# Two query heads projected between the first score fills of the next group, in the banks of the sums (layer 1 attention)

## The chip, the cores and the metric

The kernel runs on one core of one Trainium2 chip (trn2). The metric is the device time of one launch in microseconds (us). The kernel before has a median of 1783.52 us over 3 runs (1783.41 to 1785.67).

## What is computed

A network of two layers on 1024 tokens of 512 features. Layer 0 is an attention with 32 heads of 16 features and one shared key and value, beside a feed-forward part with weights from look-up tables. The change lies in layer 1, in its attention:

```
q = (x @ wq.T) as 32 heads of 128        # 8 key/value groups, 4 query heads to each
k = (x @ wk.T) as  8 heads of 128
v = (x @ wv.T) as  8 heads of 128
q = q * cos + rotate_half(q) * sin       # rotary positions, k likewise
scores = q k^T / sqrt(128), scaled by key in the first 128 keys, causal
attn = softmax(scores) @ v
out = attn @ wo.T                        # added to the input, with a gated feed-forward part behind it
```

All in float32. A matrix product is made of three products of a high and a low part of each operand (`products`, line 68).

## The kernel before

Layer 1's attention (`layer1`, line 1171) goes through the 8 key/value groups one after the other; queries come in 8 tiles of 128 tokens, heads in 2 pairs. A written list of steps sets the order of the work, and every engine walks the same list (`walk`, line 1250), each doing its own part of a step: `first_steps` (line 1138) once, then `group_steps(True)` (line 1105) seven times in a hardware loop, then `group_steps(False)`. Each engine works its own queue in order and waits on semaphores.

The steps that matter here are these, with the engines that carry them.

- `proj` f (line 1338): one of 12 projections of a group, 128 rows of weights by 512 tokens, 12 matmuls on TensorE (PE). f 0 and 1 are the key, 2 and 3 the value, 4 to 11 the four query heads, two halves of the tokens each. The result lies in PSUM bank f % 4. VectorE (DVE) rotates it (`rope`, lines 1519 to 1535: three operations that read the bank, then a sum in SBUF); GpSimd (POOL) splits the sum into a high and a low part (`rotated`, lines 1598 to 1621) and counts `kq_ready`. For the value, ScalarE (ACT) copies the bank instead (line 1467).
- `vturn` (line 1428): four transposes of the value on PE, split by ACT and DVE.
- `qk` n (line 1363), called `qknext` where it belongs to the next group: one fill of scores, for one tile and one head. Fill n lies in the two banks from 2 * (n % 2) on, so scores use banks 0 to 3 in turn, as the projections do. DVE takes the maximum (line 1546; for tile 0 a product and a maximum, lines 1549 and 1551), ACT the exponential (line 1503), DVE the reciprocal of the sum (line 1583), POOL the scaling (lines 1648 and 1649).
- `turn`, `av` (lines 1394 and 1406): probabilities are transposed in banks 4 and 5 and multiplied with the value; the sums lie in banks 6 and 7.
- `out` (line 1418): the output product of one tile, added to the residual by DVE (line 1576).
- `w`, `wo`: POOL splits a chunk of weights that the SyncE queue has loaded (line 1591).

ACT and DVE do what follows a score fill two steps late (`late_step`), POOL its scaling too. The first six score fills of the next group, n = 0 to 5, are tile 7 heads 0 and 1, tile 0 heads 0 and 1, tile 7 heads 2 and 3. At the end of a group the list read: projections 0 to 5 spread in the last pair of tiles but one, 6 to 11 in the last pair, then `out`, both `vturn`, six `qknext`, `out`. What a score fill waits for:

```
if n >= 2:
    pe.wait_ge(exp_ready, g * NHEADS + (n - 1))
else:
    pe.wait_ge(rope_read, g * 10 + 10)
    pe.wait_ge(vt_ready, g * 2 + 2)
pe.wait_ge(kq_ready, g * 10 + (2 * h + 4))
```

`exp_ready` says that the exponential has read the two banks, `rope_read` that rotations have read theirs, `kq_ready` that the rotated and split halves are there: fills of head h need 2 * h + 4 of the group's ten.

Of the kernel before, what the change touches and what calls it, by code (L numbers as in the profile page):

```python
# [25 lines left out]
ST, DT, BLK = S // P, D // P, 512  # L26
# [41 lines left out]
def products(pe, out, left, right, first, last):  # L68

    (lh, ll), (rh, rl) = left, right  # L70
    pe.matmul(out, lh, rh, start=first, stop=False)  # L71
    pe.matmul(out, lh, rl, start=False, stop=False)  # L72
    return pe.matmul(out, ll, rh, start=False, stop=last)  # L73
# [1024 lines left out]
AHEAD = 3  # L1098
NPAIR, NUNIT, NHEADS = len(PAIRS), len(UNITS), 2 * len(PAIRS)
NCHUNK, NFILL = 2 + G1, NB * (2 + G1)  # L1100
ROT_STEPS = 4 + 9
NTOK = len(PAIRS) // 2


def group_steps(more):

    turns = [("turn", u) for u in range(NUNIT)]
    main = [[] for _ in PAIRS]
    for u, (j, k) in enumerate(UNITS):
        main[j].append(("av", u))  # L1110
        if u + 2 < NUNIT:
            main[j].append(turns[u + 2])
    out = [("wo", i) for i in range(G1)] + turns[:2]
    for j in range(NPAIR):
        side = []
        if j + AHEAD < NPAIR:
            side += [("qk", 2 * (j + AHEAD)), ("qk", 2 * (j + AHEAD) + 1)]
        q, r = divmod(j, 4)
        if r == 0 and q:
            side.insert(0, ("out", 2 * q - 2))  # L1120
            side.insert(2, ("out", 2 * q - 1))
        if more and 4 <= j < 4 + W_RING:
            side.append(("w", j - 4))
        if more and j >= NPAIR - 2:
            half = NFILL // 2
            for f in range((j - NPAIR + 2) * half, (j - NPAIR + 3) * half):
                side.append(("proj", f))
                if f % NB == NB - 1 and f // NB + W_RING < NCHUNK:
                    side.append(("w", f // NB + W_RING))
        out += interleave(main[j], side)  # L1130
    out.append(("out", NTOK - 2))
    if more:
        out += [("vturn", 0), ("vturn", 1)] + [("qknext", n) for n in range(2 * AHEAD)]
    out.append(("out", NTOK - 1))
    return out


def first_steps():

    out = [("w", c) for c in range(W_RING)]  # L1140
    for f in range(NFILL):
        out.append(("proj", f))
        if f % NB == NB - 1 and f // NB + W_RING < NCHUNK:
            out.append(("w", f // NB + W_RING))
    return out + [("vturn", 0), ("vturn", 1)] + [("qknext", n) for n in range(2 * AHEAD)]


BANK_KINDS = ("turn", "vturn", "out")
# [22 lines left out]
def layer1(nc, a, keep):  # L1171
    ctx = ExitStack()
    with ctx:
# [3 lines left out]
        def sem(name):  # L1177
            return ctx.enter_context(nc.semaphore(name))

        resid, xth, xtl = keep["resid"], keep["xth"], keep["xtl"]  # L1180
        identf, identb, masku = keep["identf"], keep["identb"], keep["masku"]
        ps = ctx.enter_context(nc.psum_tensor("ps1", [P, 8, 512], F32))

        def bank(b):
            return ps[:, b % 8, :]
# [26 lines left out]
        proj_filled, rope_read, vt_ready = sem("proj_filled"), sem("rope_read"), sem("vt_ready")  # L1212
# [4 lines left out]
        o_high, o_low, y_added = sem("o_high"), sem("o_low"), sem("y_added")  # L1217
# [9 lines left out]

        def length(j):
            return PAIRS[j][0] + 1

        def pbuf(n):

# [39 lines left out]
        def split_count(s, g):  # L1272

            if isinstance(g, int) and g < 0:
                return place_first.split[s]
            return g * SPLIT_GROUP + (SPLIT_FIRST + place_of(g).split[s])
# [58 lines left out]
        def _(pe):  # L1335
            norm.tensor(nc, pe, range(EARLY))

            def proj(f, g):
                c, b = divmod(f, NB)
                if isinstance(g, int) and g == 0 and f == 1:  # L1340
                    norm.tensor(nc, pe, range(EARLY, ST))
                    pe.wait_ge(norm.low_ready, ST)
                if f < 4:
                    if isinstance(g, int) and g == 0:
                        if f == 0:
                            pe.wait_ge(norm.low_ready, ST // NB)
                    else:
                        pe.wait_ge(exp_ready, g * NHEADS)
                elif f < 6:
                    pe.wait_ge(rope_read, g * 10 + (f - 3))  # L1350
                elif f < 8:
                    pe.wait_ge(vt_ready, g * 2 + (f - 5))
                else:
                    pe.wait_ge(rope_read, g * 10 + (f - 5))
                if b == 0:
                    pe.wait_ge(w_split, g * CHUNKS + (c + 1))
                for d in range(DT):
                    w = (wh[:, c % W_RING, d * P:(d + 1) * P], wl[:, c % W_RING, d * P:(d + 1) * P])
                    last = products(pe, bank(f % 4), w, (xth[:, d, b * BLK:(b + 1) * BLK], xtl[:, d, b * BLK:(b + 1) * BLK]),
                                    d == 0, d == DT - 1)  # L1360
                last.then_inc(proj_filled, 1)

            def qk(n, g):
                j, i = divmod(n, 2)
                t, p = PAIRS[j]
                h = 2 * p + i
                if n >= 2:
                    pe.wait_ge(exp_ready, g * NHEADS + (n - 1))
                else:
                    pe.wait_ge(rope_read, g * 10 + 10)  # L1370
                    pe.wait_ge(vt_ready, g * 2 + 2)
                pe.wait_ge(kq_ready, g * 10 + (2 * h + 4))
                q = (qth[:, h, t * P:(t + 1) * P], qtl[:, h, t * P:(t + 1) * P])
                out = qk_banks(n)
                width = (t + 1) * P
                for c0 in range(0, width, BLK):
                    w = max(2 * P, min(BLK, width - c0))
                    k = (k0h[:, 0:w], k0l[:, 0:w]) if t == 0 else (kth[:, c0:c0 + w], ktl[:, c0:c0 + w])
                    products(pe, out[:, c0:c0 + w], q, k, True, c0 + BLK < width)
                pe.matmul(out[:, t * P:(t + 1) * P], identb[:], masku[:], start=False, stop=True).then_inc(qk_filled, 1)  # L1380

            def bank_free(s, g):
# [6 lines left out]
                if past[0] == "out":  # L1389
                    pe.wait_ge(y_added, g * NTOK + (past[1] + 2 - (0 if i >= 2 else NTOK)))  # L1390
                else:
# [14 lines left out]
            def av(u, g):  # L1406
                j, k = UNITS[u]
                t = PAIRS[j][0]
                if k == 0:
                    pe.wait_ge(o_low, g * NPAIR + max(1, j))  # L1410
                pe.wait_ge(low_ready, split_count(("turn", u), g) + 1)
                for kk in range(k, min(k + 2, t + 1)):
                    c = 2 * P * (kk - k)
                    last = products(pe, ps[:, 6 + j % 2, 0:2 * P], (vh[:, kk, :], vl[:, kk, :]),
                                    (ptnh[:, u % PT_RING, c:c + 2 * P], ptnl[:, u % PT_RING, c:c + 2 * P]), kk == 0, kk == t)
                last.then_inc(av_unit, 1)
# [92 lines left out]
        def _(dve):  # L1509
# [9 lines left out]
            def rope(f, g):  # L1519

                gg = g + 1
                r = f if f < 2 else f - 2
                c = HD1 ** -0.5 if f >= 4 else 1.0
                dve.wait_ge(proj_filled, gg * NFILL + (f + 1))
                if r >= 2 or not isinstance(gg, int):
                    dve.wait_ge(kq_ready, gg * 10 + (r - 1))
                cols = slice(f % NB * BLK, (f % NB + 1) * BLK)
                src = bank(f % 4)
                nc.vector.scalar_tensor_tensor(out=rota[:, r % 2, :], in0=src, scalar=c, in1=cos[:, cols], op0=ALU.mult, op1=ALU.mult)
                nc.vector.scalar_tensor_tensor(out=rotb[0:64, r % 2, :], in0=src[64:128, :], scalar=c, in1=sin[64:128, cols],  # L1530
                                               op0=ALU.mult, op1=ALU.mult)
                nc.vector.scalar_tensor_tensor(out=rotb[64:128, r % 2, :], in0=src[0:64, :], scalar=c, in1=sin[0:64, cols],  # L1532
                                               op0=ALU.mult, op1=ALU.mult).then_inc(rope_read, 1)
                dve.wait_ge(rope_read, gg * 10 + (r + 1))
                nc.vector.tensor_tensor(rota[:, r % 2, :], rota[:, r % 2, :], rotb[:, r % 2, :], ALU.add).then_inc(rotated_ready, 1)
# [53 lines left out]
        def _(pool):  # L1589
# [8 lines left out]
            def rotated(f, gg):  # L1598
# [9 lines left out]
                def chained(ins, n):  # L1608
                    ins.then_inc(rot_step, 1)
                    pool.wait_ge(rot_step, gg * ROT_STEPS + (base + n))  # L1610

# [521 lines left out]
```

## Time and profile before

| | |
|---|---|
| runs, median (lowest to highest) | 1783.52 us (1783.41 to 1785.67) |
| the profiled execution's own time | 1786.48 us |
| its span, first to last instruction | 1784.4 us |
| mean granted TensorE clock | 0.971 |
| PE busy | 1653.3 us (93%) |
| DVE busy | 1122.4 us (63%) |
| POOL busy | 812.6 us (46%) |
| ACT busy | 708.3 us (40%) |

The profiled execution took 2.08 us more than its span, and 2.96 us more than the median of the runs. PE's busy share counts a matmul from its start to the modelled end of its result, so successive matmuls overlap. Where an engine sat idle, a row of the trace says in square brackets for how long and whose instruction released it.

### The profile page before, as it was taken

Reading aid. Unit: us, or ns where it says so; the run is one execution under the profiler, and the core shown is the slowest. Engines: PE = TensorE matmul, PEld = TensorE weight load, DVE = VectorE, ACT = ScalarE, POOL = GpSimd, SP = SyncE. Lnnn points to the kernel's source line nnn. Section 1 sums busy time; section 2 is a strip of 40 time slices with the busy share of each in tenths; the row PEclk is TensorE's granted clock in tenths of the full one; section 3 lists DMA queues with packets and bytes.
Section 4 is the critical chain, followed back from the end, with each engine's and each line's share of the span. In section 5 each row is a group of like instructions: output and inputs, shape, how many; then the busy total and the mean of one; then the engine's idle time right before and its main releaser. Section 6 shows DMA issues by size and latency. Waiting matters only on the chain. (4 is left out here: it accounts for less than half of the span.)

```text
span 1784.4 us, 32078 instructions
## 1 busy us (share of the span) xinstructions
PE 1653.3 (93%) x10959; PEld 1276.0 (72%) x10959; DVE 1122.4 (63%) x1951; ACT 708.3 (40%) x1483; POOL 812.6 (46%) x806
## 2 busy tenths in 40 slices
PE   6767999999789999999999999999999999989999
PEld 4433444448568878878878878878878878867887
DVE  7867788604666676676576576576676676644333
ACT  4424556671135335325325325425325415432221
POOL 4089999100463363364364354355255264234331
PEclk9878999999899999999999999999999999989999
DMA  6540000000210000001001001001001002012101
GB/s 127 61 59 3 2 2 2 2 8 7 69 30 19 13 25 25 12 19 30 10 17 35 3 17 42 1 19 42 1 19 36 7 18 54 1 48 61 47 14 48
DMA packets 36417, 47.08 MB, mean 26 GB/s; under 512 B 12117, under 2 KB 18485, under 8 KB 36261
## 3 DMA queue, kind: packets, MB, share of 16 engines
q1 hardware_dynamic: 36282, 45.11, 10.6%
q8 instruction: 105, 1.72, 0.4%
q14 instruction: 30, 0.25, 0.0%
HBM read 37.56 MB, written 2.10 MB: 22 GB/s over the span
## 5 line engine op out<-in xcount | busy, mean ns | idle before, releaser
L1558 DVE TENSOR_TENSOR ptnl<-ps,ptnh 128x512 fp32r<-128x512 f32 (+1 forms) x320 | 203.8, 637 | 135.8 <-ACT ptnh L1476 130.1
L1476 ACT ACTIVATE ptnh<-ps 128x512 fp32r<-128x512 f32 (+1 forms) x320 | 177.6, 555 | 268.3 <-PE ps L1402 265.1
L71 PE MATMUL ps<-xth,wh 128*128 128x512 f32 (+1 forms) x560 | 225.5, 403 | 5.7 <-POOL wl L2019 4.1
L73 PE MATMUL ps<-xth,wl 128*128 128x512 f32 (+1 forms) x560 | 222.6, 398 | 0.0
L72 PE MATMUL ps<-xtl,wh 128*128 128x512 f32 (+1 forms) x560 | 222.4, 397 | 0.0
L904 DVE TENSOR_REDUCE negm<-ps 128x1 f32<-128x256 f32 (+12 forms) x224 | 178.2, 819 | 59.1 <-PE ps L473 51.3
L1546 DVE TENSOR_REDUCE negm<-ps 128x1 f32<-128x768 f32 (+3 forms) x224 | 183.4, 819 | 33.8 <-PE ps L1380 31.1
L71 PE MATMUL ps<-ptnh,vh 128*128 128x256 f32 x576 | 183.8, 319 | 10.3 <-DVE ptnl L1558 9.8
L715 ACT ACTIVATE pt<-ps 128x512 f32<-128x512 f32 x226 | 131.4, 597 | 91.8 <-PE ps L506 63.8
L73 PE MATMUL ps<-ptnh,vl 128*128 128x256 f32 x576 | 161.3, 280 | 0.0
L72 PE MATMUL ps<-ptnl,vh 128*128 128x256 f32 x576 | 160.7, 279 | 0.0
L1648 POOL TENSOR_SCALAR pshort<-pshort,rinv 128x128 f32<-128x128 f32 (+3 forms) x64 | 34.1, 532 | 275.2 <-DVE rinv L1583 275.2
L1075 POOL TENSOR_SCALAR onehot<-idx,lutl 128x512 f32<-128x512 bf16 x64 | 127.8, 1997 | 69.3 <-DVEq L890 62.9
L71 PE MATMUL ps<-kth,qth 128*128 128x512 f32 (+2 forms) x352 | 140.1, 398 | 5.0 <-DVE rot L1532 2.7
L1648 POOL TENSOR_SCALAR plong<-plong,rinv 128x1024 f32<-128x1024 f32 (+3 forms) x64 | 61.4, 960 | 178.1 <-DVE rinv L1583 178.1
L1503 ACT ACTIVATE plong<-ps,negm 128x1024 f32<-128x1024 f32 (+3 forms) x128 | 121.9, 952 | 43.8 <-DVE negm L1546 42.7
L1402 PE MATMUL ps<-identf,plong 128*128 128x128 f32 x832 | 128.7, 274 | 4.0 <-DVE resid L1576 2.1
L506 PE MATMUL ps<-qstack,kstack 124*128 124x512 bf16 x288 | 108.8, 397 | 24.9 <-DMA qstack<-mrows 21.9
L71 PEld LDWEIGHTS ps<-xth,wh 128*128 128x128 f32 (+1 forms) x560 | 106.4, 190 | 28.9 <-DVE hid L1974 2.4
L71 PEld LDWEIGHTS ps<-ptnh,vh 128*128 128x128 f32 x576 | 109.7, 191 | 22.5 <-DVE ptnl L1558 16.9
L73 PE MATMUL ps<-kth,qtl 128*128 128x512 f32 (+2 forms) x352 | 125.8, 357 | 0.0
L72 PE MATMUL ps<-ktl,qth 128*128 128x512 f32 (+2 forms) x352 | 125.5, 357 | 0.0
(227 smaller groups left out, 3838.8 us busy)
## 6 DMA issues: line engine op xcount, KB each, us to landing
raw<-in_w SPq DMA_DIRECT2D x48, 256.0 KB, 2.6
raw<-in_wo SPq DMA_DIRECT2D x32, 256.0 KB, 2.6
qstack<-qpart SPq DMA_DIRECT2D x40, 128.0 KB, 7.0
raw<-in_gate_main SPq DMA_DIRECT2D x10, 256.0 KB, 2.7
raw<-in_up_main SPq DMA_DIRECT2D x10, 256.0 KB, 2.8
raw<-in_down_main SPq DMA_DIRECT2D x10, 256.0 KB, 2.7
resid<-in_x SPq DMA_DIRECT2D x4, 512.0 KB, 5.4
out<-resid SPq DMA_DIRECT2D x8, 256.0 KB, 2.0
```

Of the source, the lines that this page charges most:

```text
L71: pe.matmul(out, lh, rh, start=first, stop=False)
L72: pe.matmul(out, lh, rl, start=False, stop=False)
L73: return pe.matmul(out, ll, rh, start=False, stop=last)
L506: last = pe.matmul(out, kstack[0:T_ROWS, tri(t) + kt * P:tri(t) + (kt + 1) * P], q, start=True, stop=kt != t)
L715: nc.scalar.activation(pt[:, m % PT0, :], ps[:, score_bank(m, t), :], ACT.Exp).then_inc(exp_done, 1)
L904: nc.vector.tensor_reduce(negm[:, t % 2, bass.ds(h, 1)], ps[:, m_bank(t, j):m_bank(t, j) + 4 // m_slots(t), :].rearrange("p b c -> p (b c) ...
L1075: nc.gpsimd.tensor_scalar(onehot[:], idx[:, ot * D:(ot + 1) * D], float(c), lutl[:, ot, c:c + 1], ALU.is_equal, ALU.mult).then_inc(hot_mad ...
L1402: last = nc.tensor.transpose(ps[:, b, (2 * (kk - k) + i) * P:(2 * (kk - k) + i + 1) * P], pbuf(2 * j + i)[:, kk * P:(kk + 1) * P], identf[:])
L1476: nc.scalar.activation(ptnh[:, i % PT_RING, 0:w], ps[:, b, 0:w], ACT.Copy).then_inc(high_ready, 1)
L1503: nc.scalar.activation(pbuf(n), src, ACT.Exp, bias=negm[:, n:n + 1], accum_out=rowsum[:, n:n + 1]).then_inc(exp_ready, 1)
L1546: nc.vector.tensor_reduce(negm[:, i:i + 1], qk_banks(i)[:, 0:(t + 1) * P], AX.X, ALU.max, negate=True).then_inc(max_ready, 1)
L1558: nc.vector.tensor_tensor(ptnl[:, i % PT_RING, 0:w], ps[:, b, 0:w], ptnh[:, i % PT_RING, 0:w].bitcast(F32), ALU.subtract).then_inc(low_rea ...
```

## The change

The projections of the third and fourth query head (f = 8 to 11) leave the spread in the last two pairs of tiles; the eight that stay are spread four and four. The four go between the first score fills of the next group, and their results go to banks 6 and 7, in which the sums of `av` lie, with f % 2. The score fills 0 and 1 wait only for the rotations that read their own banks, and the first two `av` of a group wait for the ten rotations. `rope` reads the new banks; the rest follows from the list.

```
+NFIRST = NFILL - 4

+def last_projections():
+    out = [("qknext", 0), ("vturn", 0), ("proj", NFIRST), ("vturn", 1)]
+    for n in range(1, 4):
+        out += [("qknext", n), ("proj", NFIRST + n)]
+    return out + [("qknext", n) for n in range(4, 2 * AHEAD)]
...
-            half = NFILL // 2
+            half = NFIRST // 2
...
-        out += [("vturn", 0), ("vturn", 1)] + [("qknext", n) for n in range(2 * AHEAD)]
+        out += last_projections()
...
+        def proj_bank(f):
+            return ps[:, f % 4 if f < NFIRST else 6 + f % 2, :]
...
                 elif f < 8:
                     pe.wait_ge(vt_ready, g * 2 + (f - 5))
+                elif f < NFIRST + 2:
+                    pe.wait_ge(o_low, g * NPAIR + 1)
                 else:
-                    pe.wait_ge(rope_read, g * 10 + (f - 5))
+                    pe.wait_ge(rope_read, g * 10 + (f - 3))
...
                 else:
-                    pe.wait_ge(rope_read, g * 10 + 10)
-                    pe.wait_ge(vt_ready, g * 2 + 2)
+                    pe.wait_ge(rope_read, g * 10 + (2 * n + 4))
...
                     pe.wait_ge(o_low, g * NPAIR + max(1, j))
+                    if j < 2:
+                        pe.wait_ge(rope_read, g * 10 + 10)
```

`first_steps` is changed alike: projections 0 to 7, then `last_projections`.

On PE, at the end of a turn of the loop, the fifth score fill (n = 4) stood behind the fourth. Before (L1380 is the mask that ends a fill, L71 to L73 the three products):

```order
L1380 MATMUL ps<-masku,identb 128x128
L1368 REGISTER_ALU
L1372 REGISTER_ALU [waits exp_ready]
L71 MATMUL ps<-kth,qth 128x512 [waits kq_ready]
L72 MATMUL ps<-ktl,qth 128x512
L73 MATMUL ps<-kth,qtl 128x512
L71 MATMUL ps<-kth,qth 128x512
L72 MATMUL ps<-ktl,qth 128x512
L73 MATMUL ps<-kth,qtl 128x512
L1380 MATMUL ps<-masku,identb 128x128
L1368 REGISTER_ALU
L71 MATMUL ps<-kth,qth 128x512 [waits kq_ready,exp_ready]
```

Of the change, the same place:

```order
L73 MATMUL ps<-xth,wl 128x512
L1383 REGISTER_ALU
L71 MATMUL ps<-kth,qth 128x512 [waits kq_ready,exp_ready]
L72 MATMUL ps<-ktl,qth 128x512
L73 MATMUL ps<-kth,qtl 128x512
L71 MATMUL ps<-kth,qth 128x512
L72 MATMUL ps<-ktl,qth 128x512
L73 MATMUL ps<-kth,qtl 128x512
L1394 MATMUL ps<-masku,identb 128x128
L1383 REGISTER_ALU
L1386 REGISTER_ALU [waits exp_ready]
L71 MATMUL ps<-kth,qth 128x512 [waits kq_ready]
```

The last matmul of projection 11 now stands directly ahead of fill 4, and fill 5, whose `kq_ready` counts all ten halves, is one fill behind it.

On DVE, the rotation of projection 11 was followed by the residual, the two halves of the value and the first maxima. Before, from the rotation's last operation on:

```order
L1535 TENSOR_TENSOR rot<-rot 128x512 [waits rope_read]
L1574 REGISTER_ALU
L1576 TENSOR_TENSOR resid<-ps,resid 128x512 [waits y_added,bank_filled]
L1553 REGISTER_ALU
L1562 TENSOR_TENSOR vl<-ps,vh 128x512 [waits bk_high]
L1553 REGISTER_ALU
L1562 TENSOR_TENSOR vl<-ps,vh 128x512 [waits bk_high]
L1544 ISA
L1546 TENSOR_REDUCE negm<-ps 128x1 [waits qk_filled]
L1544 REGISTER_ALU
L1546 TENSOR_REDUCE negm<-ps 128x1 [waits qk_filled]
```

Of the change, from the last operation of the rotation of projection 10 to that of projection 11:

```order
L1551 TENSOR_TENSOR rot<-rot 128x512 [waits rope_read]
L1560 REGISTER_ALU
L1565 TENSOR_TENSOR pshort<-ps,tscale 128x128 [waits qk_filled]
L1566 ISA
L1567 TENSOR_REDUCE negm<-pshort 128x1 [waits max_step]
L1540 REGISTER_ALU
L1545 SCALAR_TENSOR_TENSOR rot<-ps,raw 128x512 [waits kq_ready,proj_filled]
L1546 SCALAR_TENSOR_TENSOR rot<-ps,raw 64x512
L1548 SCALAR_TENSOR_TENSOR rot<-ps,raw 64x512
L1550 REGISTER_ALU
L1551 TENSOR_TENSOR rot<-rot 128x512 [waits rope_read]
```

The product and the maximum of fill 3 now stand between these two rotations, and four of the six fills' maxima ahead of the last rotation.

## Rows read from the trace of the kernel before

**Rows 1.** The page: busy time (share of the span) and instructions of each engine.
```profile
PE 1653.3 (93%) x10959; PEld 1276.0 (72%) x10959; DVE 1122.4 (63%) x1951; ACT 708.3 (40%) x1483; POOL 812.6 (46%) x806
```

**Rows 2.** Waits of PE in one turn of the loop: us in total, times, longest.
```profile
PE ps L71 <- ACT plong L1503: 1.9, 2, 1.0
PE ps L71 <- DVE ptnl L1558: 0.7, 2, 0.4
PE ps L1433 <- DVE resid L1576: 0.7, 1, 0.7
PE ps L1402 <- DVE resid L1576: 0.3, 1, 0.3
```

**Rows 3.** Timeline of PE at that turn's end: start, us, instruction [idle before <-releaser].
```profile
642.43 0.60 PE L1433 MATMUL ps<-identf,rot 128*128 128x128 f32 x4
643.68 0.66 PE L1433 MATMUL ps<-identf,rot 128*128 128x128 f32 x4 [0.65 <-DVE resid L1576]
644.09 0.48 PE L71 MATMUL ps<-kth,qth 128*128 128x512 f32 x1
...
648.35 0.39 PE L71 MATMUL ps<-k0h,qth 128*128 128x256 f32 x1 [1.04 <-ACT plong L1503]
...
649.87 0.39 PE L71 MATMUL ps<-k0h,qth 128*128 128x256 f32 x1 [0.82 <-ACT plong L1503]
...
650.37 0.47 PE L71 MATMUL ps<-kth,qth 128*128 128x512 f32 x1
...
651.88 0.48 PE L71 MATMUL ps<-kth,qth 128*128 128x512 f32 x1
...
656.29 0.60 PE L1402 MATMUL ps<-identf,plong 128*128 128x128 f32 x4
```

**Rows 4.** Timeline of DVE and POOL there: projection 11's rotation, its split, a scaling.
```profile
640.18 0.68 DVE L1529 SCALAR_TENSOR_TENSOR rot<-ps,raw 128x512 f32<-128x512 f32 x1
...
642.29 0.73 DVE L1535 TENSOR_TENSOR rot<-rot 128x512 f32<-128x512 f32 x1
...
643.25 0.62 POOL L1620 TENSOR_SCALAR qth<-rot 128x512 fp32r<-128x512 f32 x1 [0.77 <-DVE rot L1535]
...
643.95 1.30 POOL L1621 TENSOR_TENSOR qtl<-rot,qth 128x512 fp32r<-128x512 f32 x1
...
651.49 1.12 POOL L1648 TENSOR_SCALAR plong<-plong,rinv 128x1024 f32<-128x1024 f32 x1 [6.25 <-DVE rinv L1583]
```

**Rows 5.** Timeline of DVE: what follows a fill of tile 0.
```profile
649.08 0.29 DVE L1549 TENSOR_TENSOR pshort<-ps,tscale 128x128 f32<-128x128 f32 x1 [0.51 <-PE ps L1380]
...
649.40 0.29 DVE L1551 TENSOR_REDUCE negm<-pshort 128x1 f32<-128x128 f32 x1
```

**Rows 6.** Timeline of PE at another turn's end: first transposes of value and probabilities.
```profile
1186.21 0.60 PE L1433 MATMUL ps<-identf,rot 128*128 128x128 f32 x4
...
1201.58 0.60 PE L1402 MATMUL ps<-identf,plong 128*128 128x128 f32 x4
```

**Rows 7.** Stretches: us, busy time by engine, granted clock (PEclk), DMA share, GB/s.
```profile
507.70:511.50 3.80, 3.80 (x13) 2.74 (x12) 2.22 (x3) 1.20 (x2) 1.28 (x2) 0.55 0.00 0
522.40:526.00 3.60, 3.60 (x30) 3.56 (x31) 1.62 (x3) 1.20 (x2) 3.52 (x5) 1.00 0.02 5
1193.00:1197.00 4.00, 3.38 (x10) 2.44 (x10) 1.09 (x5) 1.50 (x6) 1.47 (x2) 0.60 0.00 0
```

**Rows 8.** Timeline of PE ahead of the loop: projection 8, value, first score, first sum.
```profile
491.35 0.39 PE L71 MATMUL ps<-xth,wh 128*128 128x512 f32 x1
...
502.50 1.04 PE L1433 MATMUL ps<-identf,rot 128*128 128x128 f32 x8
...
506.20 0.50 PE L71 MATMUL ps<-kth,qth 128*128 128x512 f32 x1 [2.67 <-DVE rot L1532]
...
522.39 0.39 PE L71 MATMUL ps<-ptnh,vh 128*128 128x256 f32 x1 [2.88 <-DVE ptnl L1558]
```

**Rows 9.** Timeline of DVE: one sum of a rotation that took longer than its like.
```profile
630.11 1.56 DVE L1535 TENSOR_TENSOR rot<-rot 128x512 f32<-128x512 f32 x1
```

More of the change, by code:

```diff
@@ L1140, in first_steps @@
     out = [("w", c) for c in range(W_RING)]
-    for f in range(NFILL):
+    for f in range(NFIRST):
         out.append(("proj", f))
@@ L1144, in first_steps @@
             out.append(("w", f // NB + W_RING))
-    return out + [("vturn", 0), ("vturn", 1)] + [("qknext", n) for n in range(2 * AHEAD)]
+    return out + last_projections()
 BANK_KINDS = ("turn", "vturn", "out")
@@ L1358, in proj @@
                     w = (wh[:, c % W_RING, d * P:(d + 1) * P], wl[:, c % W_RING, d * P:(d + 1) * P])
-                    last = products(pe, bank(f % 4), w, (xth[:, d, b * BLK:(b + 1) * BLK], xtl[:, d, b * BLK:(b + 1) * BLK]),
+                    last = products(pe, proj_bank(f), w, (xth[:, d, b * BLK:(b + 1) * BLK], xtl[:, d, b * BLK:(b + 1) * BLK]),
                                     d == 0, d == DT - 1)
@@ L1527, in rope @@
                 cols = slice(f % NB * BLK, (f % NB + 1) * BLK)
-                src = bank(f % 4)
+                src = proj_bank(f)
                 nc.vector.scalar_tensor_tensor(out=rota[:, r % 2, :], in0=src, scalar=c, in1=cos[:, cols], op0=ALU.mult, op1=ALU.mult)
```

## Prediction

> **What bounds the kernel now.** Read the page first: TensorE is busy for 93% of the span, no other engine for more than 63% [rows 1], and its mean granted clock is 0.971 of full. So time is gained only where PE stands still or its clock falls. Then PE's waits over one turn of the group loop: of some 136 us ((1186.21 - 642.43) / 4 [rows 3, 6]) the three largest sorts take 3.3, 1.9 for ACT's exponential and 0.7 twice for DVE [rows 2]. The timeline of the turn's end shows where they lie: the second `vturn` waits 0.65 us for the residual, score fills 2 and 3 wait 1.04 and 0.82 us for the exponentials that must read their banks [rows 3]. These are what the moved projections could fill.
>
> **What is removed, in each of seven turns.** From the first `vturn` (642.43) to fill 4 (650.37) PE spends 7.94 us [rows 3]. The work in it, by start-to-start times of the same rows: eight transposes at 0.41 a four (643.68 to 644.09), 0.82; fills 0 and 1 like fill 4, 1.51 (650.37 to 651.88), 3.02; fills 2 and 3 at 0.50 (649.87 to 650.37), 1.00. Together 4.84, so the stalls cost 3.10 us, a little over the 2.51 that the brackets show because a result's last part no longer overlaps the next matmul. With a projection of 2.79 us ((502.50 - 491.35) / 4 [rows 8]) ahead of each of fills 1 to 4 the maxima and exponentials are done in time, and the residual long before the second `vturn`. I take the whole 3.10 as gone; at least the 0.82 of the single wait on fill 3 must go, since its cover alone is 2.79.
>
> **What is added: fill 5 waits for the last projection.** Fill 5 is tile 7 of head 3 and needs all ten halves rotated and split. Projection 11 was followed on PE by an output product, two `vturn` and five fills; now only fill 4 stands between. The chain from projection 11 is in the rows: its rotation starts on DVE at 640.18, its sum ends at 643.02, POOL takes it up 0.23 later at 643.25 and ends the low half at 645.25, in all 5.07 us [rows 4]. To it come 0.16 us from PE's last issue slot to the end of its result (a matmul of 0.39 us issued 0.23 apart, 2.79 / 12), about 0.2 for the hand-offs from PE to DVE and from POOL to PE (an estimate by the 0.23 from DVE to POOL), and DVE's lateness. DVE has between the two last projections a rotation of 2.84 and the two short operations on fill 3, 0.61 [rows 5], 3.45 in all, against 0.50 + 2.79 = 3.29 on PE: late by about 0.1 to 0.2. Sum 5.07 + 0.16 + 0.2 + 0.1 = 5.5; fill 4 covers 1.51. **The new wait is 4.0 us.** At the least it is 3.7 (no lateness, hand-offs of nothing), at the most 4.8 (below, the collision). Queued behind it on PE are fill 5, the last `out` and the whole next group; nobody can pass.
>
> Waits: 4.0 - 3.10 = +0.9 us a turn, times 7 = **+6.3**, with 3.7 and 4.8 **+4.2 to +11.9**, as far as the old stalls go whole.
>
> **The clock.** In the turn at 1186 the granted clock was 0.60 over four microseconds [rows 7], part of it at the lower of the two levels, 1.2 GHz, after the same stalls of about 1 us; the stretch from the first `vturn` to the next group's first transposes took 15.37 us against 13.86 in the turn at 642 [rows 3, 6], so a fall costs 1.51. One turn in seven shows it. Ahead of the loop PE stood 2.67 us, and the clock was 0.55 right after; after another stand of 2.88 us it was 1.00 [rows 7, 8]. A single wait of 4.0 us is longer than all of these, so I take a fall in six turns of seven, five more than now: **+7.5**. Bounds: no fall at all, -1.5; in all seven, +9.1. [...]
>
> **Ahead of the loop.** From projection 8's start to the first `av` the kernel takes 31.04 us (491.35 to 522.39 [rows 8]). Its work: four projections 11.15, eight transposes 0.82, six fills 7.04, two `turn` 0.82, 19.8; the rest is waits and a clock that falls there. Afterwards the same stretch begins right behind projection 7: fill 0's halves are split while projections 6 and 7 run, so 19.8, the 4.0 for fill 5, and some 3.2 ahead of the first `av`, which hangs on fill 5's exponential in ACT's queue, as it did (2.88 and the unoverlapped part): 27.0. One or two falls of 1.51 bring 28.5 or 30.0. Against 31.04 that is -2.5 to -1.0; with two long waits there I take **-1.5**, bounds -3 and 0.
>
> **At no cost.** The `turn` and `av` of the last two pairs lose two projections each as cover; four stay in each, 11.2 us against a round trip whose stalls elsewhere are 0.4 at most [rows 2]. If it failed, 0.4 a turn. POOL's scaling of the first pair, 2 x 1.12 [rows 4], now stands between the splits of projections 9 and 10; the split of 10 ends some 0.8 late, but 11's sum arrives about 0.5 after that. Projection 8 waits for sums read before projection 6's rotation. Weight chunks, DMAs and matmuls are as many as before.
>
> **Sum.** 6.3 + 7.5 - 1.5 = +12.3 us; all low ends together give -0.3, all high ends +21.0. The profiled execution has a span of 1784.4 and 2.08 around it: 1786.48 becomes 1798.8. That execution is 2.96 above the median of the runs, so the forecast for the median is 1783.52 + 12.3 = **1795.8**. Changes below 0.2% (3.6 us) can't be told from none.
>
> **Rivals.** (1) *The clock holds.* The wait comes but the chip lets the clock stand, as after the 2.88 us [rows 8]: 6.3 - 1.5 with at most one fall as now, 1788, between no change and slower. For it speaks that one row, against it the two falls after shorter stands.
> (2) *A collision of DVE and POOL.* One sum in SBUF took 1.56 us [rows 9] instead of 0.73 [rows 4]; I take it that it met POOL's low half, which works on SBUF too. Rotation 11's sum meets the end of POOL's split of 10; if it waits out a whole such operation, each chain is 0.83 longer: +5.8, 1802. By the order above the overlap is only about 0.3.
> (3) *Faster: the wait is paid back.* While PE stands 4.0 us, ACT, DVE and POOL clear what they are behind, and the stalls early in the next group vanish. Those are 1.0 us in three waits, for `ptnl` and the residual [rows 2], with unoverlapped parts of 0.2 each (as 3.10 against 2.51 above) 1.6. It decides where more than 0.7 a turn comes back and no more turns fall (6.3 - 1.5 over seven); with all of it 1783.5 + 6.3 - 1.5 - 11.2 = 1777. Against it: those are round trips from PE over ACT and DVE back to PE [rows 2], which start after the wait and are not arrears.
>
> **Chances and range.** Forecast with most turns falling 0.68, clock holds 0.14, collision 0.10, paid back 0.08. The forecast's own span is 1790 to 1799. The range takes in half of rival 1 and the nearer part of rival 2: **1786.5 to 1801**. Faster is rival 3, 0.08; within 0.2% (up to 1787.1) is the better part of rival 1, 0.12; slower is 0.80.
>
> **What would show it.** Right: in each turn PE's L71 of a fill sits idle some 3.7 us released by POOL's low half of a query, the exponential's 1.9 and the residual's 0.65 are gone from PE's waits, and the granted clock is under 1 behind most of these waits. Wrong: a wait at fill 5 well under 3 us, or a full clock behind it.

## The result, and the profile after

| | before | after |
|---|---|---|
| runs side by side, median (lowest to highest) | 1783.95 us (1783.41 to 1785.67) | 1809.81 us (1807.22 to 1810.72) |
| ratio of the two over all runs, 95% interval | | 1.0141 (1.0123 to 1.0158) |
| the profiled execution's own time | 1786.48 us | 1809.05 us |
| its span | 1784.4 us | 1807.3 us |
| mean granted TensorE clock | 0.971 | 0.964 |

The change costs 25.9 us, where 12.3 were forecast: slower, as said, but twice as much, and 1809.81 lies above the range.

The page of the kernel after, busy time of each engine, shows no new work: the counts of instructions are the same. POOL and DVE gain 3.4 and 1.6 us, and some of their instructions do take longer where they meet (below); PE gains 6.7 us net, with matmuls that last longer at the lower clock [rows 1].

```profile
PE 1660.0 (92%) x10959; PEld 1284.2 (71%) x10959; DVE 1124.0 (62%) x1951; ACT 709.1 (39%) x1483; POOL 816.0 (45%) x806
```

PE's waits in one turn of the loop of the kernel after (us in total, times, longest) answer to rows 2. The exponential's 1.9 and the residual's 0.7 ahead of the second `vturn` are gone, as forecast. (The 0.2 for `pshort` is one in the middle of the group, which stood there before, too.) In their place stands one wait of 4.4 for POOL's low half of a query, alike in all seven turns.

```profile
PE ps L71 <- POOL qtl L1637: 4.4, 1, 4.4
PE ps L71 <- DVE ptnl L1574: 0.8, 2, 0.4
PE ps L1416 <- DVE resid L1592: 0.3, 1, 0.3
PE ps L71 <- ACT pshort L1519: 0.2, 1, 0.2
PE ps L1416 <- POOL plong L1665: 0.2, 1, 0.2
```

The timeline of PE at a turn's end of the kernel after, from fill 4 (start, us, instruction, idle before and its releaser), shows both halves of the price. Fill 5 starts 4.43 us late, and its first matmul takes 0.80 instead of the 0.48 of [rows 3]. From fill 5 to the next group's first transposes pass 6.95 us (1069.90 to 1076.85), where the kernel before needed 4.41 (651.88 to 656.29 [rows 3]) for the same fill and `out`. The wait is the same in all seven turns; that second stretch takes 5.99 us in the first turn and 6.78 to 7.01 in the others.

```profile
1063.84 0.40 PE L71 MATMUL ps<-kth,qth 128*128 128x512 f32 x1
...
1065.24 0.23 PE L1394 MATMUL ps<-masku,identb 128*128 128x128 bf16 x1
1069.90 0.80 PE L71 MATMUL ps<-kth,qth 128*128 128x512 f32 x1 [4.43 <-POOL qtl L1637]
1070.50 0.63 PE L72 MATMUL ps<-ktl,qth 128*128 128x512 f32 x1
...
1072.72 0.78 PE L71 MATMUL ps<-woh,oth 128*128 128x512 f32 x1
...
1076.85 0.60 PE L1416 MATMUL ps<-identf,plong 128*128 128x128 f32 x4
1077.80 0.66 PE L1416 MATMUL ps<-identf,plong 128*128 128x128 f32 x4 [0.35 <-DVE resid L1592]
```

Stretches of the kernel after (us, busy time by engine, granted clock, DMA share, GB/s) say why. PE is never idle from 1069.90 to 1076.90, and yet the granted clock is 0.60; over the first five microseconds it is 0.50, which is the lower of the two levels, 1.2 GHz, throughout. It was 0.50 already over the last microsecond of the wait, in which PE did nothing.

```profile
1068.80:1069.80 1.00, 0.00 (x0) 0.00 (x0) 0.07 (x1) 0.97 (x1) 1.00 (x1) 0.50 0.00 0
1069.90:1076.90 7.00, 7.00 (x20) 5.20 (x21) 1.22 (x1) 1.33 (x4) 0.65 (x2) 0.60 0.02 5
1070.00:1075.00 5.00, 5.00 (x12) 3.61 (x13) 1.22 (x1) 0.77 (x2) 0.55 (x2) 0.50 0.03 7
```

**Where the time lies.** The two traces are laid side by side by four marks: the start of Layer 1 (its second projection, the first that stands behind all the transposes of the input, 471.72 before and 470.61 after; what lies ahead of it is called Layer 0 here), the first `av` (522.39 and 520.55), the first transposes at the end of the loop's first turn (656.29 and 657.46) and of its last (1473.58 and 1496.63).

| stretch | before | after | difference |
|---|---|---|---|
| Layer 0 | 471.72 | 470.61 | -1.1 |
| Layer 1 ahead of the loop | 50.67 | 49.94 | -0.7 |
| first turn | 133.90 | 136.91 | +3.0 |
| six turns | 817.29 | 839.17 | +21.9 |
| last group and what follows | 310.82 | 310.67 | -0.1 |

Layer 1 alone is 24.0 us longer (1336.7 against 1312.7). That is the change's price in these two executions, free of what Layer 0 does, which the change doesn't touch.

### The profile page after: what moved, and what is told of

Same layout as the page of the kernel before. It is cut to its first block and busy times, and to the rows that moved or that the text cites. A ratio compares the mean times of both kernels' runs of the same rounds, so it can differ in the third digit from the quotient of the medians.

```text
span 1807.3 us, 32113 instructions
## 1 busy us (share of the span) xinstructions
PE 1660.0 (92%) x10959; PEld 1284.2 (71%) x10959; DVE 1124.0 (62%) x1951; ACT 709.1 (39%) x1483; POOL 816.0 (45%) x806
## 3 DMA queue, kind: packets, MB, share of 16 engines
q1 hardware_dynamic: 36282, 45.11, 10.3%
## 5 line engine op out<-in xcount | busy, mean ns | idle before, releaser
L71 PE MATMUL ps<-xth,wh 128*128 128x512 f32 (+1 forms) x560 | 228.3, 408 | 5.7 <-POOL wl L2035 4.1
L73 PE MATMUL ps<-xth,wl 128*128 128x512 f32 (+1 forms) x560 | 223.0, 398 | 0.0
L71 PE MATMUL ps<-ptnh,vh 128*128 128x256 f32 x576 | 184.3, 320 | 9.2 <-DVE ptnl L1574 8.7
L71 PE MATMUL ps<-kth,qth 128*128 128x512 f32 (+2 forms) x352 | 141.0, 400 | 39.1 <-POOL qtl L1637 36.7
L73 PE MATMUL ps<-ptnh,vl 128*128 128x256 f32 x576 | 161.3, 280 | 0.0
L73 PE MATMUL ps<-kth,qtl 128*128 128x512 f32 (+2 forms) x352 | 127.8, 363 | 0.0
L71 PEld LDWEIGHTS ps<-xth,wh 128*128 128x128 f32 (+1 forms) x560 | 106.8, 191 | 28.2 <-DVE hid L1990 2.4
L71 PEld LDWEIGHTS ps<-ptnh,vh 128*128 128x128 f32 x576 | 109.7, 190 | 21.3 <-DVE ptnl L1574 16.0
```

## The experiments

One theory, that the whole loss lies between fills 4 and 5 (the wait and the clock behind it), was set against three rivals: the banks and the cover that the change took from other steps; POOL's scaling in the way of the splits; and something that no row had named. Two sets of four kernels were run, each beside the kernel before (medians 1785.18 and 1785.34). Ratios are to those. Layer 0 is the same code in all of them, yet in the profiled executions it ended anywhere from 464.05 to 471.72 us. So the length of Layer 1 in each one's profiled execution, from the mark above to the end of the span, is read beside the medians. For the kernel before it is that of the one trace of it, which was not taken beside these sets:

| kernel | median, us | against before | Layer 1, us | against before |
|---|---|---|---|---|
| before | 1785.18, 1785.34 | | 1312.7 | |
| e1_filler | 1804.96 | +19.8 | 1337.7 | +25.0 |
| e2_four_ahead | 1784.71 | -0.5 | 1311.2 | -1.5 |
| e3_out_as_cover | 1778.9 | -6.3 | 1312.3 | -0.3 |
| e4_reordered | 1762.78 | -22.4 | 1296.3 | -16.4 |
| e5_filler_in_loop | 1792.57 | +7.2 | 1322.7 | +10.0 |
| e6_eight_fillers | 1798.46 | +13.1 | 1328.2 | +15.5 |
| e7_scaling_late | 1798.91 | +13.6 | 1328.9 | +16.2 |
| e8_change_again | 1808.8 | +23.5 | 1338.8 | +26.1 |

**e1_filler: keep PE at work during the wait.** Sixteen matmuls whose result is not used stand ahead of fill 5, in the loop and ahead of it; they wait until the last rotation but one has read bank 6.

```
                 elif kind == "qknext":
+                    if i == 5:
+                        pe.wait_ge(rope_read, (g + 1) * 10 + 9)
+                        for _ in range(16):
+                            pe.matmul(bank(6), qth[:, 0, 7 * P:8 * P], kth[:, 0:BLK], start=True, stop=True)
                     qk(i, g + 1)
```

> Sixteen matmuls of 512 columns, some 3.7 us, whose result nobody uses, stand between score fills 4 and 5, in bank 6 behind the rotation that reads it; nothing else differs from the changed kernel. Theory (a wait of 4.6 us at fill 5 and, behind it, a clock at the lower level that costs 2.5 us a turn): the halves are ready when they were, fill 5 starts at the same time, but PE has been busy and the clock stays up, so 7 x 2.5 and about 1 ahead of the loop come back: 1809.8 - 19 = 1791. Rival (only the wait costs, the slow stretch is hidden or comes anyway): 1810.

Measured: 1804.96 us, ratio 1.0108 (1.008 to 1.0135), far from what was expected. The timeline of PE of e1 shows that the expected part did come: fill 5 waits 0.80, and the way to the transposes is 4.42 us (645.62 to 650.04), at the full clock. But the second four transposes then stand still for 2.09 us that the profile puts down to issue, which is to say that PE waited for nothing that it shows.

```profile
645.62 0.50 PE L71 MATMUL ps<-kth,qth 128*128 128x512 f32 x1 [0.80 <-POOL qtl L1641]
...
650.04 0.60 PE L1416 MATMUL ps<-identf,plong 128*128 128x128 f32 x4
652.73 0.66 PE L1416 MATMUL ps<-identf,plong 128*128 128x128 f32 x4 [2.09 <-issue]
```

That gap, 2.09 to 2.46 us, came six times, at each start of the loop's body but the first, and slow matmuls followed it. It took back what the fillers had saved. So e1's time does not speak to the theory; e5 asks again without the code ahead of the loop.

**e2_four_ahead: the change's banks and its 4 + 4 spread, the old place.** The list at the group's end is projections 8 to 11, `out` 6, both `vturn`, fills 0 to 5, `out` 7.

> The four projections stay in banks 6 and 7 with their new waits, and the last two pairs of tiles keep four projections each, but all four stand ahead of the output product and the score fills, none between them. Theory (the loss is fill 5's wait alone): that wait goes, the old stalls of 3.1 us a turn at the second turn of the value and at fills 2 and 3 return, a clock that falls about as rarely as before: 1784 to 1787. Rival (banks 6 and 7, or the two projections that the last pairs lost as cover, cost part of the 25.9 us): 1790 or more.

Measured: 1784.71 us, ratio 0.9994 (0.9982 to 1.0007), no difference, as expected. PE's waits in one of its turns are those of the kernel before, and one new one of 0.3, of a projection for the rotation that must read its bank.

```profile
PE ps L71 <- ACT plong L1514: 1.9, 2, 1.0
PE ps L71 <- DVE ptnl L1569: 0.8, 2, 0.4
PE ps L1444 <- DVE resid L1587: 0.5, 1, 0.5
PE ps L71 <- DVE rot L1543: 0.3, 1, 0.3
```

A turn takes 136.3 to 136.4 us, some 0.4 more than the 135.97 of before's turns without a fall. That Layer 1 is 1.5 us shorter all the same lies elsewhere: no turn has a fall, and the last group and what follows take 2.5 less. So the banks 6 and 7 and the thinner spread under the last two pairs cost at most 0.4 us a turn, under 3 of the 24. The loss is the new place among the fills.

**e3_out_as_cover: something useful behind projection 11.** The list is fill 0, `vturn` 0, projection 8, fill 1, projection 9, fill 2, projection 10, fill 3, projection 11, fill 4, `out` 6, `vturn` 1, fill 5, `out` 7.

> The changed kernel with the output product and the second turn of the value moved from ahead of the fills to between fills 4 and 5. Theory (what was short is cover behind projection 11): 3.1 us more of work stand in the wait, 4.6 falls to 1.0 to 1.6, PE's other stalls at the turn's end stay gone, and so short a wait brings a fall in no more than one or two turns of seven: 1.5 to 2 us a turn under the kernel before, 1770 to 1775. Rival (projections between the fills delay maxima and exponentials on DVE whatever stands where): 1795 to 1810.

Measured: 1778.9 us, ratio 0.9969 (0.9958 to 0.998): faster than before by the medians, if by less than expected. Layer 1 does not show a gain of that size: in its one trace it is as long as in the one of before, so where the 6.3 us lie stays open. The timeline of PE of e3 shows the wait at fill 5 down to 1.17, and why the rest was missed: `out` 6 had also covered fill 0, which now waits 1.37 for its own halves.

```profile
899.72 0.47 PE L71 MATMUL ps<-kth,qth 128*128 128x512 f32 x1 [1.37 <-POOL qtl L1632]
...
916.72 0.50 PE L71 MATMUL ps<-kth,qth 128*128 128x512 f32 x1 [1.17 <-POOL qtl L1632]
```

No turn has a fall behind the 1.17. A turn takes 135.8 to 136.0 us, as before, where the change took 139.9: the old stalls are gone, and two new waits of 2.5 together stand in their place.

**e4_reordered: cover on both sides.** The list is projection 8, fill 0, projection 9, fills 1 and 2, `vturn` 0, projections 10 and 11, fill 3, `out` 6, fill 4, `vturn` 1, fill 5, `out` 7.

> The same steps in another order: projection 8, fill 0, projection 9, fills 1 and 2, first turn of the value, projections 10 and 11, fill 3, output product, fill 4, second turn of the value, fill 5, output product. Theory: behind projection 11 stand fill 3, an output product, fill 4 and four transposes, 0.5 + 2.8 + 1.5 + 0.4 = 5.2 us against a chain of 5.5 to 6.1, so the wait at fill 5 falls to 0.3 to 0.9 and the others are gone; 2.2 to 2.8 us a turn under the kernel before: 1763 to 1769. Rival (the order shifts the wait to fills 1 or 2): 1775 or more.

Measured: 1762.78 us, ratio 0.9883 (0.9855 to 0.991), as expected and ahead of both kernels. PE's waits in one of its turns list none for a projection's split (0.1 us is idle ahead of fill 5), and 0.4 of the exponential's 1.9:

```profile
PE ps L71 <- DVE ptnl L1569: 0.8, 2, 0.4
PE ps L71 <- ACT plong L1514: 0.4, 1, 0.4
PE ps L1411 <- DVE resid L1587: 0.3, 1, 0.3
```

A turn takes 133.6 to 133.9 us against 136.0, and Layer 1 is 16.4 us shorter. Layer 0 ended 7 us earlier in this execution than in that of before; that the rest of the 22 us is its is likely, but not shown. The same four projections, in the same banks, give 16 us or take 24 by the order in which they, the fills, `out` and `vturn` stand.

**e5_filler_in_loop: e1's matmuls in the loop alone.**

```
-                    if i == 5:
+                    if i == 5 and not isinstance(g, int):
```

> The sixteen unused matmuls between fills 4 and 5 in the loop alone, so that all code ahead of the loop, and the place of the loop's start in it, are those of the changed kernel. Theory (the 2.1 us in which PE had no instructions in the first filler kernel came of where its code lay, and the clock's fall is a cost of its own): no such gap, fill 5 to the first transposes 4.4 us instead of 7.0, about 2.5 us a turn less than the changed kernel beside it, -15 to -18 us. Rival (behind the loop's jump the instructions arrive some 7 us after fill 5's release, whatever the clock does): the gap of 2 us again, 0 to -6 us.

Measured: 1792.57 us, ratio 1.0044 (1.0031 to 1.0058), and 16.2 below the change as it was run again beside it (e8), as expected. The timeline of PE of e5: 0.78 of wait is left, 4.43 us lie between fill 5 and the transposes (1062.50 to 1066.93), and no gap follows.

```profile
1062.50 0.50 PE L71 MATMUL ps<-kth,qth 128*128 128x512 f32 x1 [0.78 <-POOL qtl L1641]
...
1066.93 0.60 PE L1416 MATMUL ps<-identf,plong 128*128 128x128 f32 x4
```

Its stretch between the two marks has the full clock:

```profile
1062.50:1066.90 4.40, 4.40 (x19) 3.39 (x20) 1.22 (x1) 1.32 (x4) 0.66 (x2) 1.00 0.01 4
```

This splits the price of a turn. The fillers don't make POOL any earlier, so fill 5 starts as late as in the change, only the clock is saved. A turn of e5 takes 137.4 us. The five turns of before without a fall take 135.97 on average, the one with a fall 137.46; so the wait costs 1.43, net of the old stalls, and the one fall of before cost 1.49. Turns of the change run again (e8) take 139.9, so its falls cost 2.5.

**e6_eight_fillers: half the dose.** The same with `range(8)`.

> Eight unused matmuls instead of sixteen in the same place, 1.9 us, so PE still stands some 2.5 us ahead of fill 5. Theory (how long PE stands decides whether the clock falls): a fall in some turns, shorter than with 4.4 us, fill 5 to the first transposes 5 to 6 us in the mean, -7 to -14 us against the changed kernel beside it. Rival (any wait of a few us brings the whole fall): 0 to -4 us.

Measured: 1798.46 us, ratio 1.0075 (1.005 to 1.0099), 10.3 below e8, as expected. Fill 5 waits 2.60 in every turn, but the clock fell in only four of the seven. Two stretches of e6 from fill 5 on, one turn apart, show it: 1.00 in the one, 0.72 in the other, behind the same wait.

```profile
787.70:792.20 4.50, 4.46 (x20) 3.26 (x20) 1.23 (x1) 1.37 (x4) 0.69 (x2) 1.00 0.01 4
925.20:931.20 6.00, 5.95 (x19) 4.43 (x20) 1.23 (x1) 1.38 (x4) 0.71 (x2) 0.72 0.02 5
```

Turns without a fall take 137.4 us, turns with one 139.0, so a fall behind this wait costs 1.6. And the first matmul of fill 5 still takes 0.50 in all seven: where the clock falls, it does so a little later than in the change.

**e7_scaling_late: POOL's scaling out of the way.** The scaling of the first pair of fills is put behind the split of projection 11 instead of ahead of that of projection 10.

```
                     rotated(i, gg)
+                    if i == NFILL - 1:
+                        scale("qknext", 1, g)
...
-                kind, n = s
+                if s != ("qknext", 1):
+                    scale(*s, g)
```

> POOL scales the probabilities of the first pair behind the split of projection 11 instead of ahead of the split of projection 10; nothing else differs from the changed kernel. Theory (the wait is 4.4 us and not 3.8 because the rotation sums of projections 10 and 11 met this scaling and the late split, 1.24 and 0.91 us instead of 0.69): sums of 0.69, fill 5 waits 3.7 to 3.9, 0.5 to 0.7 us a turn less, -3 to -5 us against the changed kernel beside it, with the clock falling as before. Rival (DVE's own order makes it late): the wait stays over 4.2, 0 to -1 us.

Measured: 1798.91 us, ratio 1.0076 (1.0049 to 1.0102), 9.9 below e8 and so about twice the expected gain. The wait itself came out as expected, as PE's waits in one turn of e7 show:

```profile
PE ps L71 <- POOL qtl L1637: 3.7, 1, 3.7
```

The timeline of DVE of e7 shows the sums of the rotations 10 and 11 at their undisturbed time:

```profile
1057.83 0.69 DVE L1551 TENSOR_TENSOR rot<-rot 128x512 f32<-128x512 f32 x1
...
1061.08 0.69 DVE L1551 TENSOR_TENSOR rot<-rot 128x512 f32<-128x512 f32 x1
```

The shorter wait (4.46 in e8) is worth 7 x 0.79 = 5.5 of the 9.9. Most of the rest is clock: a fall still came in every turn, but the seven stretches from fill 5 to the transposes take 5.85 to 7.20 us instead of 6.89 to 6.98 in e8, together 3.1 less. So a fall costs 1.4 to 2.8 here. Another 0.8 is the same wait's, ahead of the loop (3.78 instead of 4.58).

**e8_change_again: the change beside e5 to e7.**

> The changed kernel again, for comparison on the same chip. Both theories: 1.2% to 1.6% over the kernel before, a turn of 139.7 to 140.0 us.

Measured: 1808.8 us, ratio 1.0128 (1.0094 to 1.0163), with a wait of 4.46 in its turns of 139.9 us. The first result holds.

## Why the forecast was right in direction and wrong in size

**The old stalls: right.** All 3.10 us a turn went. The waits of after hold no exponential of fills 2 and 3, and no residual ahead of `vturn`; and e5, whose turns have the new wait and no fall, takes 137.4 us a turn, which is 135.97 - 3.10 + 4.55.

**The new wait: right place, right releaser, 0.5 too short.** From fill 4's start (1063.84) to fill 5's (1069.90) pass 6.06 us, less the 1.51 of fill 4's own work 4.55, where 4.0 was forecast. The step that failed is "At no cost": POOL's scaling of the first pair was said to be covered between the splits of projections 9 and 10. Without it (e7) fill 5 starts 5.30 us behind fill 4, which less 1.51 is 3.79; so the other terms were 0.2 too long, and this one, put at nothing, was worth 0.8. The timeline of DVE after, from the sum of rotation 10 to that of rotation 11, shows two sums in SBUF of 1.24 and 0.91 us instead of 0.73 [rows 4]:

```profile
1062.95 1.24 DVE L1551 TENSOR_TENSOR rot<-rot 128x512 f32<-128x512 f32 x1
1064.12 0.28 DVE L1565 TENSOR_TENSOR pshort<-ps,tscale 128x128 f32<-128x128 f32 x1
1064.42 0.29 DVE L1567 TENSOR_REDUCE negm<-pshort 128x1 f32<-128x128 f32 x1
1064.63 0.68 DVE L1545 SCALAR_TENSOR_TENSOR rot<-ps,raw 128x512 f32<-128x512 f32 x1
...
1066.75 0.91 DVE L1551 TENSOR_TENSOR rot<-rot 128x512 f32<-128x512 f32 x1
```

and the timeline of POOL after what they met:

```profile
1062.53 1.13 POOL L1664 TENSOR_SCALAR plong<-plong,rinv 128x1024 f32<-128x1024 f32 x1
1063.63 1.55 POOL L1665 TENSOR_SCALAR plong<-plong,rinv 128x1024 f32<-128x1024 f32 x1
1065.16 0.61 POOL L1636 TENSOR_SCALAR qth<-rot 128x512 fp32r<-128x512 f32 x1
1065.85 1.26 POOL L1637 TENSOR_TENSOR qtl<-rot,qth 128x512 fp32r<-128x512 f32 x1
1067.88 0.62 POOL L1636 TENSOR_SCALAR qth<-rot 128x512 fp32r<-128x512 f32 x1 [0.77 <-DVE rot L1551]
1068.58 1.26 POOL L1637 TENSOR_TENSOR qtl<-rot,qth 128x512 fp32r<-128x512 f32 x1
```

Read it as a chain. Rotation 10's sum starts while POOL's first scaling runs, and takes 1.24. The second scaling starts while that sum runs, and takes 1.55 instead of 1.12. So DVE begins rotation 11 at 1064.63, 0.79 behind fill 4, where at most 0.36 had been allowed (0.16 and half the hand-offs and lateness of 0.1). POOL begins the split of 10 late, and its low half, ending at 1067.11, meets rotation 11's sum, which takes 0.91. Then all goes as costed: 0.22 to POOL, 1.96 for the split, 0.06 to PE. e7 took the scaling away, and both sums fell to 0.69 and the wait to 3.67. This is what rival 2 described, only that it had named the split of 10 alone. The Trainium skill (SBUF — State Buffer, Who interferes with whom) says that a DVE instruction with two inputs in SBUF contends with a GpSimd instruction that reads SBUF, for a pair of ports that one holds while the other stands. The trace agrees: if each of the three long instructions waited for the end of the other and then took its undisturbed time (0.69, 1.12, 0.69), they would end at 1064.35, 1065.31 and 1067.80; they end at 1064.19, 1065.18 and 1067.66. In microseconds: the wait was forecast at +6.3 over seven turns and came to 7 x 1.43 = +10.0.

**The clock: the term that was mis-sized.** The step was "a fall costs 1.51", in six turns of seven, five more than before. That price came from the turn at 1186, where stalls of about 1 us with matmuls between them stood ahead of the fall [rows 6, 7]. Behind one stand of 4.43 us the clock was low from fill 5's first matmul on (0.79 or 0.80 us in six turns, 0.50 in the first as in e5 at the full clock) and stayed low for 5.5 us, to the `out` matmul at 1075.43. And it fell in seven turns of seven. The stretches from fill 5 to the transposes add up to 47.6 us, seven of 4.42 without a fall to 30.9; the falls cost 16.7, or +15.2 less the 1.49 of the one fall of before, where +7.5 was forecast and +9.1 was the upper bound. Rival 1, that the clock holds, failed in every turn. The Trainium skill (TensorE: Matmul & The Clock Gate, What's actually happening) lets equal waits fare differently, since the stretches over which the chip watches the engine run free of the program. Behind the 2.60 of e6 they did; behind the 3.67 of e7 and the 4.43 of the change every turn fell.

**Ahead of the loop: right sign, half the size.** -0.7 where -1.5 was forecast.

**Sum.** 10.0 + 15.2 - 0.7 = 24.5, against 24.0 in Layer 1's length. Of the 12.2 us by which that sum exceeds the forecast, 7.7 are the clock's, 3.7 the wait's and 0.8 the stretch ahead of the loop. The medians' 25.9 hold 1.9 more than Layer 1, which leaves Layer 0 and the scatter of the runs (the profiled execution of before lay 2.5 above its median, that of after 0.8 below).

**Rival 3, the wait paid back: fell.** The 0.7 for `ptnl` and the 0.3 for the residual early in the next group [rows 2] stand after as before, at 0.8 and 0.3.

## What to carry to other kernels

When a producer is moved closer to its consumer, add up the whole chain between them (rotation, sum, split, hand-offs) and put that much other work of the same engine behind it: here 1.5 us stood where 6 were needed, and moving the same four projections so that fills, `out` and `vturn` lie behind them turned a loss of 24 us in Layer 1 into a gain of 16 (e4). The long, undivided wait on TensorE was charged twice here, once as idle time (1.43 us a turn, net of the old stalls) and once as slow matmuls behind it (about 2.4); the second charge has to be read from stands of its own length, not from shorter ones. Work called covered on a second engine must also be looked at for what it shares with the chain, here DVE's sums and POOL's scaling in SBUF.

## What the runs showed of the hardware that was not expected

The second charge is not in proportion to the wait. Behind 0.78 us at fill 5 (e5) no turn fell, nor behind 1.17 to 1.22 (e3); behind 2.60 (e6) four of seven did, at 1.6 us each; behind 3.67 (e7) all seven, at 1.4 to 2.8; behind 4.43 all seven, at 1.6 in the first and 2.4 to 2.6 in the others. In e5 and e6 the unused matmuls stand ahead of the wait, in e7 and the change fill 4 alone, so more than the wait's length differs between them. What sets the length of the low stretch was not settled.

With sixteen more matmuls ahead of the loop (e1) TensorE stood 2.1 to 2.5 us at each return to the start of the loop's body, behind the first four transposes, without any releaser; with the same matmuls in the loop alone (e5) it never did. Where the loop's instructions came to lie is the likely difference, but this was only argued: no run moved the code by itself.

Layer 0, untouched, ended as much as 7.7 us apart in the profiled executions: at 464.05 to 464.61 in e1 to e4, at 467.75 to 469.59 in e5 to e8, at 470.61 and 471.72 in the first two. The granted clock over it was 0.94 in e1 to e3 and 0.92 in the longest, so falls of the clock are likely a part of it; why they differ is open. A gain of a few us in the median, like e3's, need not come from the change that is tested; the marks of the stretch that was changed help to tell, and a trace of the kernel before from the same set would be needed to be sure.
